# A two-block transformer kernel on one core: four staging tiles for the weights of the opening, small loads moved to SyncE, and a new order of the first batch

## What is computed

```python
xn = _layernorm(x, axis=-1)
x = x + _L0_attn_ref(xn, ...) + _L0_ffn_ref(xn, ...)   # 16 heads, ALiBi, causal; 8 experts, silu(x Wg) * (x Wu) @ Wd, weighted by a router
xn = _layernorm(x, axis=-1)
x = x + _L1_attn_ref(xn, ...) + _L1_ffn_ref(xn, ...)   # 16 heads, causal; ternarized W1 and W2, gelu, 4-bit fake quantization of the whole output
```

## Time and profile before

| | |
|---|---|
| median of three runs | 767.87 us (767.48 to 768.92) |
| the profiled execution | 767.54 us, its span 765.6 us |
| PE busy | 650.1 us, 85% of the span |
| DVE busy | 564.8 us, 74% |
| ACT busy | 465.8 us, 61% |
| POOL busy | 268.8 us, 35% |
| mean TensorE clock granted | 0.948 |

### The profile page before, as it was taken

The page is one execution under the profiler, slowest core; times in us unless marked ns, Lnnn a source line. Parts: engine busy times, 40 slices in busy tenths (PEclk is TensorE's granted clock), DMA queues, the critical chain, the costliest instruction groups (busy, mean ns, idle before and its releaser), DMA issues.

```text
span 765.6 us, 19944 instructions
## 1 busy us (share of the span) xinstructions
PE 650.1 (85%) x6455; PEld 482.5 (63%) x6455; DVE 564.8 (74%) x2201; ACT 465.8 (61%) x1223; POOL 268.8 (35%) x386
## 2 busy tenths in 40 slices
PE   1476777989889997999899997999799988999854
PEld 1354565767666775777676776677577766767522
DVE  4479777886688859796779758795879668886364
ACT  2558756955379355965398436946487436954533
POOL 7836541223404241243313331324213341134335
PEclk9979797999999999999999999999999998999969
...
GB/s 210 262 127 118 7 62 64 107 6 36 111 5 110 14 110 27 110 0 68 82 55 55 14 110 27 110 14 92 45 78 31 24 114 1 111 3 15 172 173 83
DMA packets 49539, 56.72 MB, mean 74 GB/s; under 512 B 5088, under 2 KB 40032, under 8 KB 49504
## 3 DMA queue, kind: packets, MB, share of 16 engines
...
q10 hardware_dynamic: 1984, 1.21, 0.6%
...
## 4 chain that ended last, share of the span: by engine, by line
PE 57%; DVE 14%; ACT 13%; issue 8%; DMA 3%; ACTq 1%; SPq 1%; POOL 1%; DVEq 1%; POOLq 0%
PE gen_ps L1138 16%; PE gen_ps L1149 9%; PE gen_ps L1111 6%; PE value_ps L1253 5%; PE gen_ps L1180 3%; PE gen_ps L1169 3%; ACT probs L1013 3%; ACT hid L1001 3%; PE value_ps L1259 2%; DVE probs L1524 2%; PE score_ps L1193 2%; DVE probs L1549 2%; DMA gu_lo<-x_dram 2%; PE turn_ps L1222 2%; PE turn_ps L1203 1%
## 5 line engine op out<-in xcount | busy, mean ns | idle before, releaser
L856 POOL TENSOR_TENSOR h_lo<-hid,h_hi 128x512 f16<-128x512 f32 x64 | 74.5, 1164 | 280.4 <-ACT h_hi L994 280.4
L1013 ACT ACTIVATE probs<-probs,nmax 128x256 f32<-128x256 f32 (+1 forms) x256 | 113.5, 447 | 25.6 <-DVE nmax L1524 25.1
L1138 PE MATMUL gen_ps<-xe_hi,gu_hi 128*128 128x256 f16 x512 | 101.8, 282 | 2.2 <-issue 2.2
L1138 PE MATMUL gen_ps<-xe_lo,gu_hi 128*128 128x256 f16 x512 | 101.6, 282 | 0.0
L1138 PE MATMUL gen_ps<-xe_hi,gu_lo 128*128 128x256 f16 x512 | 101.5, 281 | 0.0
L1524 DVE CUSTOM_DVE_ANT_0 probs<-score_ps,bias 128x256 f32<-128x256 f32 (+1 forms) x256 | 79.4, 352 | 16.1 <-PE score_ps L1195 15.4
L1538 DVE CUSTOM_DVE_ANT_0 junk<-score_ps,bias 128x256 bf16<-128x256 f32 (+1 forms) x256 | 76.0, 354 | 20.5 <-PE score_ps L1195 17.8
L1041 ACT ACTIVATE et<-turn_ps 128x384 f32<-128x384 f32 x128 | 55.7, 489 | 46.9 <-PE turn_ps L1228 42.9
L990 ACT ACTIVATE tanh_sb<-gen_ps 128x512 f32<-128x512 f32 x64 | 37.9, 591 | 70.9 <-PE gen_ps L1138 70.9
L1549 DVE TENSOR_SCALAR probs<-probs,rsum 128x256 f32<-128x256 f32 (+1 forms) x256 | 76.4, 341 | 4.5
L865 POOL TENSOR_SCALAR_AFFINE_SELECT et<-et 128x256 f32<-128x256 f32 x128 | 50.8, 419 | 67.5 <-ACT et L1041 67.4
...
## 6 DMA issues: line engine op xcount, KB each, us to landing
...
```

Of the source, the lines that this page charges most:

```text
L856: pool.tensor_tensor(h0_lo[:, e], hid0[:, e], h0_hi[:, e], ALU.subtract).then_inc(s_h0l, 1)
L1013: last = act.activation(probs[:, k, lo:hi], probs[:, k, lo:hi], ACT.Exp, scale=-1.0, bias=nmax[:, k, j:j + 1], accum_out=esum[:, k, j:j + 1])
L1138: last = pe.matmul(g[:, S * f:S * f + S], w[:, st.arg, m, k, cols], xx[:, k, :], start=(i == 0), stop=(i == len(terms) - 1))
```

## The change

There are four staging tiles. The two new ones lie in one tile `stack1`, which from now on also holds block 1's q and k stacks. The load of split i waits for the low part of split i - 4, and SP issues the first four tiles before its first step. ACT keeps four of its twelve loads (the small ones of block 0 and its v weights); the other eight are issued by SP, one behind the second weight tile and seven behind the fourth. The setup of block 1's small tables becomes a step of its own, `setup:3`, with a semaphore of its own for each half. `up` on PE now waits for the same things as `gate`, since `up:0` may stand ahead of `gate:0`. The order of the opening is new on all engines. The orders of the other passes are the same words broken into lines elsewhere, and are left out here.

```diff
+RAW = 4
...
     "tensor": {
         "first": """
-            ln0a ln0b setup split xe split:1 setup:2 vsplit tr0 split:2 split:3 l0 q0 v0 split:5 k0 gate setup:1 rt1
-            v0:1 norm:1 up gate:1 score norm split:4 rt2 score:1 up:1 split:6 down score:2 turn:1 gate:2 score:3
-            split:7 norm:2 down:1 score:4 turn up:2 gate:3 score:5 norm:3 norm:4 split:9 up:3 gate:4 turn:2 split:8
-            score:6 tern down:2 norm:6 norm:5 turn:3 tmx split:10 value score:8 tern:1 turn:4 down:3 norm:7 turn:5
-            norm:8 split:11 score:7 up:4 tern:6 turn:6 score:10 score:9 norm:9 turn:7 score:11 score:12 turn:9
-            norm:11 gate:5 tern:2 down:4 norm:10 turn:8 value:1 norm:12 score:13 split:13 turn:10 tern:3 split:12
-            +ln0a tern:4 up:5 tsm gate:6 score:14 turn:11 gate:7 +ln0b up:6 down:5 norm:14 score:15 turn:12 norm:15
-            turn:13 tern:5 value:2 tmx:1 norm:13 up:7 tern:8 +tr0 vsplit:1 down:6 turn:14 tern:7 +q0 +k0 +v0 tern:9
-            +l0 turn:15 value:3 +xe +v0:1 op0 down:7 tsm:1 tern:10 tern:11
+            norm setup ln0a tr0 q0 vsplit split setup:3 k0 up v0 gate setup:2 split:1 l0 gate:1 norm:2
+            split:4 score:2 v0:1 split:12 setup:1 split:11 split:10 rt2 up:1 ln0b split:6 down gate:2 score
+            score:3 norm:1 up:2 rt1 turn:1 score:4 norm:5 down:1 gate:3 split:8 turn +ln0a score:8 norm:6
+            turn:2 score:5 score:6 xe split:5 tmx up:3 norm:11 tern:1 score:1 down:3 tern:6 gate:4 norm:3
+            split:7 turn:4 score:10 turn:6 value split:9 split:2 norm:15 down:2 norm:10 split:3 norm:7
+            tern:2 turn:3 turn:7 score:9 score:13 norm:12 norm:13 up:4 turn:5 score:14 score:12 +l0 turn:8
+            norm:4 vsplit:1 turn:10 tern:5 score:11 down:4 gate:5 tern:4 norm:9 turn:9 value:1 turn:11
+            score:7 norm:14 up:5 tsm gate:6 gate:7 norm:8 tern turn:13 up:6 score:15 turn:12 down:5 up:7
+            +tr0 tern:8 tmx:1 +q0 down:6 +k0 +v0 value:2 turn:15 turn:14 +ln0b value:3 op0 down:7 tern:3 +xe
+            tern:7 tern:10 +v0:1 tern:9 split:13 tsm:1 tern:11
...
     "scalar": {
         "first": """
-            split:1 split vsplit tr0 split:2 q0 split:3 k0 gate v0 v0:1 split:5 split:4 gate:1 up score rt2 score:1
-            split:6 split:7 gate:2 up:1 score:2 score:3 turn turn:1 split:8 score:4 gate:3 up:2 split:9 turn:2
-            score:5 up:3 turn:3 score:6 split:10 gate:4 score:7 turn:5 turn:4 split:11 turn:6 score:8 up:4 score:11
-            turn:7 score:10 score:9 turn:8 score:12 gate:5 value:1 split:12 score:13 turn:9 turn:10 tern:4 up:5
-            split:13 turn:11 gate:6 score:14 gate:7 up:6 turn:12 turn:13 score:15 vsplit:1 +tr0 turn:14 +q0 +k0
-            turn:15 value:3 up:7 +v0:1 +v0 tern:10
+            vsplit split:6 split split:1 tr0 q0 k0 split:4 gate:1 split:5 v0:1 gate score v0 split:3 up rt2
+            score:3 up:1 split:8 split:7 turn:1 gate:2 score:4 score:2 split:9 turn:6 split:10 score:11
+            gate:3 up:2 turn:4 score:6 split:2 score:7 up:3 turn:3 score:8 turn:7 score:5 gate:4 split:12
+            split:11 turn:9 turn:10 turn:2 score:10 score:13 up:4 score:15 turn:8 turn score:12 gate:5
+            score:1 turn:5 tern:4 turn:14 split:13 gate:7 up:6 turn:11 gate:6 vsplit:1 up:5 turn:13 score:9
+            +tr0 up:7 +q0 +k0 value:1 score:14 turn:15 turn:12 +v0:1 value:3 tern:10 +v0
...
     "vector": {
         "first": """
-            ln0a split setup ln0b split:1 vsplit tr0 setup:2 split:2 v0 l0 gate rt1 v0:1 up split:4 gate:1 score
-            score:1 up:1 norm rt2 norm:2 split:6 score:2 down gate:2 score:3 norm:1 score:4 down:1 norm:3 up:2
-            split:8 gate:3 score:5 norm:4 up:3 tern score:6 norm:5 tmx tern:1 gate:4 score:7 down:2 split:10 score:8
-            norm:6 norm:7 down:3 score:9 up:4 norm:8 score:11 score:10 norm:9 score:12 norm:11 tern:2 gate:5 down:4
-            score:13 +ln0a up:5 norm:10 norm:12 split:12 tsm tern:5 tern:6 score:14 gate:6 norm:13 up:6 +ln0b
-            score:15 gate:7 down:5 tmx:1 norm:15 vsplit:1 norm:14 +tr0 up:7 down:6 tern:8 tern:7 +l0 +v0 +v0:1 op0
-            down:7 tsm:1 tern:11
+            ln0a split ln0b setup setup:2 split:4 tr0 vsplit l0 v0 gate up setup:3 score:1 split:1 rt1
+            gate:1 up:1 score:3 v0:1 split:2 rt2 split:6 score:4 norm:2 score norm:6 down gate:2 down:1 tern
+            norm:3 score:6 score:2 up:2 norm tmx score:5 gate:3 score:7 up:3 norm:7 split:10 norm:4 score:10
+            down:2 norm:1 score:8 down:3 gate:4 score:9 score:11 norm:10 up:4 norm:5 tern:1 score:12 norm:12
+            tern:2 norm:9 norm:8 score:13 down:4 +ln0a gate:5 split:8 norm:13 up:5 split:12 norm:11 tsm
+            tern:6 +ln0b score:14 gate:6 tern:5 up:6 gate:7 down:5 up:7 tmx:1 +tr0 score:15 norm:15 tern:8
+            tern:7 +l0 vsplit:1 norm:14 down:6 op0 +v0 tsm:1 +v0:1 down:7 tern:11
...
     "gpsimd": {
         "first": """
-            ln0a xe split:3 setup:1 split:5 up up:1 split:7 up:2 split:9 up:3 tern split:11 up:4 tern:3 +ln0a up:6
-            split:13 up:5 tern:11 up:7 +xe tern:9
+            ln0a xe split:3 setup:1 up:3 split:5 tern up:1 split:11 up:4 up:2 split:7 up tern:3 +ln0a
+            split:13 up:6 split:9 up:7 tern:9 up:5 +xe tern:11
...
-        q_stack = [[sb(f"q_stack{l}{u}", [2 * KR, H // 4, S], F16) for u in range(2)] for l in range(2)]
-        k_stack = [[sb(f"k_stack{l}{u}", [2 * KR, H // 4, S], F16) for u in range(2)] for l in range(2)]
+        q_stack = [[sb(f"q_stack{l}{u}", [2 * KR, H // 4, S], F16) for u in range(2)] for l in range(1)]
+        k_stack = [[sb(f"k_stack{l}{u}", [2 * KR, H // 4, S], F16) for u in range(2)] for l in range(1)]
+        stack1 = sb("stack1", [2 * KR, 2, 2, H // 4, S], F16)
+        q_stack.append([stack1[:, u, 0] for u in range(2)])
+        k_stack.append([stack1[:, u, 1] for u in range(2)])
...
+        raw += [stack1[:, u].rearrange("p a h n -> p (a h n)").bitcast(F32) for u in range(2)]
...
-                if i >= 2:
-                    sp.wait_ge(*lo_done(i - 2))
-                dst, (what, a) = raw[i % 2], SPLIT[i]
+                if i >= RAW:
+                    sp.wait_ge(*lo_done(i - RAW))
+                dst, (what, a) = raw[i % RAW], SPLIT[i]
...
-                if name == "split" and st.arg + 2 < len(SPLIT):
-                    load_raw(st.arg + 2)
+                if name == "split" and st.arg + RAW < len(SPLIT):
+                    load_raw(st.arg + RAW)
...
             load_x(Index(None, 0))
             load_raw(0)
             load_raw(1)
+            sp.dma_start(slope_sb[:], slopes.partition_broadcast(P)).then_inc(s_c, 16)
+            load_raw(2)
+            load_raw(3)
+            sp.dma_start(ob[0][:], ob0.partition_broadcast(P)).then_inc(s_ob, 16)
+            sp.dma_start(bqk[1][:], bqk1).then_inc(s_c, 16)
+            sp.dma_start(vb[1][:], vb1.partition_broadcast(P)).then_inc(s_c, 16)
+            sp.dma_start(wv_raw[1].rearrange("p (k n) -> p k n", k=NK), wv1.rearrange("(k p) n -> p k n", p=P)).then_inc(s_wv[1], 16)
+            sp.dma_start(ob[1][:], ob1.partition_broadcast(P)).then_inc(s_ob, 16)
+            sp.dma_start(b1_sb[:], b1c).then_inc(s_c, 16)
+            sp.dma_start(b2_sb[:], b2.partition_broadcast(P)).then_inc(s_c, 16)
...
-            for l, bias in enumerate((ob0, ob1)):
-                act.dma_start(ob[l][:], bias.partition_broadcast(P)).then_inc(s_ob, 16)
-            small = [(bqk[0][:], bqk0), (half_t[:], temp.partition_broadcast(P)), (vb[0][:], vb0.partition_broadcast(P)),
-                     (slope_sb[:], slopes.partition_broadcast(P)), (bqk[1][:], bqk1), (vb[1][:], vb1.partition_broadcast(P)),
-                     (b1_sb[:], b1c), (b2_sb[:], b2.partition_broadcast(P))]
-            for l, w in enumerate((wv0, wv1)):
-                act.dma_start(wv_raw[l].rearrange("p (k n) -> p k n", k=NK),
-                              w.rearrange("(k p) n -> p k n", p=P)).then_inc(s_wv[l], 16)
-            for dst, src in small:
-                act.dma_start(dst, src).then_inc(s_c, 16)
-            assert NC == len(small)
+            act.dma_start(bqk[0][:], bqk0).then_inc(s_c0, 16)
+            act.dma_start(half_t[:], temp.partition_broadcast(P)).then_inc(s_c0, 16)
+            act.dma_start(vb[0][:], vb0.partition_broadcast(P)).then_inc(s_c0, 16)
+            act.dma_start(wv_raw[0].rearrange("p (k n) -> p k n", k=NK), wv0.rearrange("(k p) n -> p k n", p=P)).then_inc(s_wv[0], 16)
...
-                    act.wait_ge(s_raw[i % 2], 16 * sum(2 if what == "gu" else 1 for what, _ in SPLIT[i % 2:i + 1:2]))
-                    act.activation(split_parts(i)[0], raw[i % 2], ACT.Copy, scale=WSCALE).then_inc(s_hi, 1)
+                    act.wait_ge(s_raw[i % RAW], 16 * sum(2 if what == "gu" else 1 for what, _ in SPLIT[i % RAW:i + 1:RAW]))
+                    act.activation(split_parts(i)[0], raw[i % RAW], ACT.Copy, scale=WSCALE).then_inc(s_hi, 1)
```

(20 more changed lines are left out.)

118 lines of the change are left out of this document (63 added, 55 removed).

## The result

| | before | after |
|---|---|---|
| median | 767.67 us (767.14 to 768.92) | 789.61 us (787.59 to 792.44) |
| the profiled execution, its span | 767.54, 765.6 us | 788.76, 787.0 us |
| DVE busy ahead of pass 1 | 81.14 us | 96.94 us |
| POOL busy ahead of pass 1 | 68.46 us | 67.45 us |

The changed kernel is slower, 1.0293 of the time before [1.0258, 1.0327]: about 22 us, where 2.5 had been forecast.

The account below looks back on a forecast made before the run. DVE was taken to bound the opening: 96.4 us without idle time, plus 3.5, 2.5 and 2.0, then a 17.0 tail, put pass 1 at 121.4, 2.5 later. Forecast 770.1 us, range 763 to 775 (eight times in ten).

Parts of the forecast that it names:

- start of the first score: Opening: first score starts at 34.5 us instead of 38.07, a gain of 3.6; bounds 33.5 and no gain.
- DVE's own work behind it: DVE from first score to `tern:8`: 59.3 us before, plus 4.4 moved in, less 2.3 moved out, 61.4.
- exclusion up to `tern:8`: DVE standing still beside POOL before `tern:8` ends: 3.5 us after `tern:2` plus 2.5 at `split:4` and `rt2`.
- idle time: DVE's waits between first score and `tern:8`: 2.0 us left of 9.5, bounds 0 and 5.
- tail: From the end of `tern:8` to pass 1: 17.0 us against 12.03; 14.6 if DVE's three steps precede POOL's multiply.
- pass 1's first matmul: End of the opening on PE: 121.4 us against 118.94, 2.5 later.
- three named places: DVE meets POOL after `tern:2` (3.5 us), at `split:4` and `rt2` (2.5), and in the tail (17.0 against 12.03).
- the norms behind `tern:2`: Two DVE norms there wait for POOL's 4.08 us multiply: 3.5 us more, bounds 0 and 4.1.
- `split:4` and `rt2`: These DVE steps run beside POOL's `split:5` and tables: 2.5 us more, bounds 0 and 5.
- The bounce: Stacks' way through DRAM before the first score, four stores and eight loads: the same 10.7 us as before.
- the landing of `wv0`: ACT's first step `vsplit` waits for this last of its four loads, taken to land at 9.1 us; bounds 8 and 11.
- the last rival (773): Tiles gain nothing because DVE, not ACT, is late: 5 us idle left, not 2; 773 us, no chance of its own.

Follow-up runs that it names:

- The two moves of one clash: In the changed kernel, two norms behind `tern:2` moved behind `gate:5`: 785.96 us (1.025); separately, POOL's tables moved behind `split:9`: 788.34 us (1.028).
- the first two experiments: Changed program, orders of before, `setup:3` ahead of first score: 769.71 us (1.0041); kernel before with only loads moved and `setup:3` separate, two tiles: 766.28 us (0.9973).

## Why the prediction was right and wrong

The sign and the mechanism held; the size didn't. Step by step, in us:

| term | forecast | measured | difference |
|---|---|---|---|
| start of the first score | 34.5 | 36.66 | +2.2 |
| DVE's own work behind it | 61.4 | 74.84 - 14.4 = 60.4 | -1.0 |
| exclusion up to `tern:8` | 6.0 | 14.4 | +8.4 |
| idle time (with the 0.5 ahead of DVE's first score) | 2.5 | 79.93 - 74.84 = 5.1 | +2.6 |
| tail | 17.0 | 20.90 | +3.9 |
| pass 1's first matmul | 121.4 | 137.49 | +16.1 |

**The step that failed is the exclusion.** It was priced at three named places. At the norms behind `tern:2` the price was about right, 4.6 us (forecast 3.5). At `split:4` and `rt2` it was at its upper bound, 5.0 (2.5, bounds 0 and 5), and only some 1.7 of that stood beside the tables. And 4.8 us more (14.4 less 4.6 and 5.0) stood at places that the forecast didn't name, splits and norms that ran while POOL subtracted or made the biases. The rule behind them was there, in the earlier trace rows. What was missed is that it must be summed over the whole stretch and not listed: DVE was busy 94% of it (74.84 of 79.93), and 16.5 us were lost beside POOL's 33.85, where the order before lost 2.1 beside 30.23. How much of that is the fuller DVE, and how much which steps fall beside POOL, isn't separated. The cut of POOL's steps shows the size: 21.4 us in the new order, 2.6 in the old. The two moves of one clash show that no single place holds it: part of the time came back at other pairs of steps, part as waits for PE.

**The tail** was mis-sized by 3.9 us, and little of that is exclusion. The multiply and `l0` end 5.2 us after `tern:8`, as in the sum (4.1 and 1.2; `l0`'s 4.55 us are mostly the multiply's), and `vsplit`, which met POOL's next subtraction, took 0.9 more. The rest is PE at the lower clock, a term that the sum didn't have: behind its wait of 5.03 us for the norm the last value took 1.93 us and the output projection 3.75. With POOL's steps cut short PE waited 0.94 us there, ran at 1.00 and took 1.07 and 1.97:

```profile
111.82 1.97 PE L1198 MATMUL gen_ps<-wo_sb,at 128*128 128x256 f32 x8 [0.55 <-issue]
```

From the sums to pass 1 it was then 7.60 us, against 9.49 (forecast 7.8). So some 3 of the 3.9 us are the clock, an estimate from 0.4 at the turn, 0.9 at the value and 1.9 behind the sums.

**The start.** The bounce was right (10.6 against 10.7), and so was that x is transposed less than 1 us earlier (14.56 against 14.85). Wrong was the landing of `wv0`: ACT's first step started at 10.92, not 9.1, at the upper bound of 11, and `split:0` stood behind it until 11.47. With the loads moved but `split:0` first on ACT, it starts at 6.95 and 7.41 (the first two experiments) and q0 at 13.84 and 14.14; in after q0 starts at 17.98. The score gained 1.4 us, where my walk said 3.6. The Trainium skill, Trainium Kernel Development and Optimization, section Key Constraints, says that issuing from several engines only saves issue time, and the estimate by it was 1.6: nearer, but by luck. ACT's first step starts at 10.92, no earlier than before (10.72), so none of the freed issue time reached it, and the 1.4 us came behind it.

**Idle time.** ACT hardly waits for weights any more; yet 5.1 us of DVE's idle time are left of 9.5, and 7.8 with POOL's steps cut short. The reading behind the term was off. Of ACT's waits for weight tiles only 2.2 us stood behind the first score, and of the 5.7 us of the earlier trace rows the 4.9 are the wait that ends with the first score itself. Behind it DVE waited above all for PE, 2.7 us at `hid` and 2.4 at the sums of W1. That the tiles leave 5 us was the last rival (773): it came true beside the forecast, not in its place.

**Small edits.** Passes, `up`'s waits and the memory of the new tiles show no cost, as said. One sentence was wrong: the moved loads are not first used in `setup:1`. `xb` on POOL needs both output biases, and waits 4.09 us for them in after; with four tiles ahead of them in the old order that may be part of what separates 1.0041 from 0.9973.

**The range**, 763 to 775, was too narrow because each exclusion was bounded at its own place; the upper end should have held POOL's whole time behind the first score, 33.85 us in after, beside which 16.5 came to be lost before `tern:8`.

Open: why the last piece ran at different granted clocks, what DVE would wait for in the new order without any clash, and what the program part costs.
